# One evacuation, transpose and normalisation of the cross-attention sums per pair of sequences, with two heads in 32 rows, and weight clips at another step

## What is computed

```
x = layernorm(x + self_attention(x))          # 16 heads of 16 channels, causal
x = layernorm(x + cross_attention(x, ctx))    # works across channels, see below
x = layernorm(x + ffn(x))                     # 256 -> 1024 -> 256, activations and
                                              # weights quantised, silu, gelu, layernorm
```

```
scores = einsum('bhtc,bhsc->bhts', q, k) / sqrt(8)
p_attn = softmax(scores)
out    = einsum('bhts,bhsc->bhtc', p_attn, v)      # the value sums
out    = Wo @ out + bo
```

## Time and profile before

| what | us |
|---|---|
| median of three runs | 551.99 (551.63 to 553.26) |
| the profiled execution's own time | 549.98 |
| its span in the profile | 548.1 |
| stage 1 up to the last evacuation of `u_b` | about 408 |
| stage 2 | about 140 |

### The profile page before, as it was taken

How to read it: one execution, slowest core, us unless ns; L and a number is a source line. 1 busy time by engine, 2 the same in 40 slices (tenths; PEclk the granted TensorE clock), 3 DMA queues, 4 the chain that set the end, 5 groups by cost and what they waited for, 6 DMA issues and landing times. The chain is left out here.

```text
span 548.1 us, 12074 instructions
## 1 busy us (share of the span) xinstructions
PE 438.9 (80%) x4162; PEld 237.8 (43%) x4162; DVE 446.5 (81%) x980; ACT 383.8 (70%) x716; POOL 287.9 (53%) x389
## 2 busy tenths in 40 slices
PE   6568799999999999999999999998877602555564
PEld 4354445455455564545545455443332201333342
DVE  3755787988979889798998988888739959999983
ACT  2231266678777786777877768767878878999982
POOL 5742656455565555645547465551033637767652
PEclk9676799999999999999999999999998965555555
DMA  7135327342232322414223242221000000000001
GB/s 223 48 78 175 87 56 218 93 109 69 64 109 57 101 73 62 111 50 105 69 64 99 56 111 61 64 80 51 2 2 1 2 0 0 10 30 22 27 31 38
DMA packets 51676, 37.10 MB, mean 68 GB/s; under 512 B 21408, under 2 KB 47648, under 8 KB 51488
## 3 DMA queue, kind: packets, MB, share of 16 engines
q1 hardware_dynamic: 51328, 36.10, 23.2%
q10 hardware_dynamic: 288, 0.23, 0.2%
HBM read 24.52 MB, written 10.49 MB: 64 GB/s over the span
## 5 line engine op out<-in xcount | busy, mean ns | idle before, releaser
L980 DVE TENSOR_REDUCE MX<-mx_b 128x2 f32<-128x512 f32 x256 | 167.7, 678 | 29.2 <-PE mx_b L585 28.1
L785 ACT ACTIVATE PB<-e_b 128x512 f32<-128x512 f32 x256 | 149.4, 592 | 58.6 <-PE e_b L613 57.4
L585 PE MATMUL mx_b<-KA,QA 48*128 48x256 bf16 x512 | 97.5, 275 | 12.2 <-DVE MX L980 11.5
L613 PE MATMUL e_b<-QA,KA 50*128 50x256 bf16 x512 | 96.9, 274 | 0.3 <-DMA QA<-MR 0.3
L630 PE MATMUL u_b<-PB,VA 128*32 128x256 f32 x1024 | 82.6, 391 | 2.4 <-ACT PB L785 1.5
L907 POOL TENSOR_TENSOR SP<-SP,srec 128x1024 f32<-128x1024 f32 x15 | 28.5, 1903 | 81.1 <-DVE srec L952 81.1
L585 PEld LDWEIGHTS mx_b<-KA,QA 48*128 48x128 bf16 x512 | 29.4, 94 | 87.8 <-issue 43.9
L1308 PE MATMUL r_b<-identh,Q 128*128 128x128 f16 x128 | 16.6, 311 | 39.3 <-ACT Q L1221 39.3
L1253 POOL TENSOR_TENSOR H<-H,row_tab 128x1024 f32<-128x1024 f32 x15 | 35.4, 2360 | 21.4 <-ACT H L1211 17.9
L1314 PE MATMUL z_b<-w2q,Q2T 128*128 128x256 bf16 x128 | 30.2, 418 | 19.3 <-ACT Q2T L1232 19.3
L897 POOL TENSOR_TENSOR KM<-QK,att_tab 128x512 f32<-128x512 f32 x31 | 32.0, 1054 | 20.6 <-ACT QK L739 20.6
(11 more groups left out here) (172 smaller groups left out, 1050.5 us busy)
## 6 DMA issues: line engine op xcount, KB each, us to landing
KA<-parts_k SPq DMA_DIRECT2D x64, 96.0 KB
QA<-parts_q SPq DMA_DIRECT2D x64, 96.0 KB
parts_q<-part_q SPq DMA_DIRECT2D x32, 128.0 KB, 1.9
parts_k<-part_k SPq DMA_DIRECT2D x16, 192.0 KB, 2.1
C<-in_ctx SPq DMA_DIRECT2D x16, 128.0 KB, 3.1
X<-in_x SPq DMA_DIRECT2D x16, 128.0 KB, 3.2
out_y<-O SPq DMA_DIRECT2D x16, 128.0 KB, 1.7
XT<-in_xT SPq DMA_DIRECT2D x15, 128.0 KB, 2.2
```

Of the source, the lines that this page charges most:

```text
L585: m = nc.tensor.matmul(mx_b[n % 2][:, D * k:D * k + D], QA[low:low + K_MAX, 2 * i.ring + b, h, P * u:P * u + P], KA[low:low + K_MAX, 2 * i ...
L613: m = nc.tensor.matmul(e_b[n % 2][:, D * k:D * k + D], KA[low:low + K_EXP, 2 * i.ring + b, h, P * sc:P * sc + P], QA[low:low + K_EXP, 2 * ...
L785: nc.scalar.activation(PB[:, n % 4].rearrange("p e t -> p (e t)"), e_b[n % 2][:, :], ACT.Exp, scale=XC ** -0.5).then_inc(e_sb.sem, 1)
L980: nc.vector.tensor_reduce(MX[:, b, e, 2 * q:2 * q + 2, u], mx_b[n % 2][:, :].rearrange("p (e s) -> p e s", e=2), AXL.X, ALU.max).then_inc( ...
```

## The change

Heads j and 4 + j now share the same 32 rows of `u_b`, and a sequence takes 256 columns, so that the bank holds both sequences of the pair. For that `VA` gets zeros in columns 16 to 31 of each head (8 values, 8 ones, 16 zeros). Heads 0 to 3 take their own 32 columns as lhs, and heads 4 to 7 take 32 columns that begin 16 earlier, in the zeros of the head before. All four products of a head pair accumulate into the same place. `u_copy`, `u_transpose` and `u_norm` run once a pair, at step 0, 3 and 3 of the next turn, with a reciprocal of 32 and a product of 256 elements per partition. The channel order of the value bias and of the output weights is permuted on the host to match. The clips of turn 7's pieces and so on stand at step 1 of the following turn, all four together.

```diff
-        RD = sb("RD", [P, 16])
+        RD = sb("RD", [P, 32])
...
-        def u_transpose(pe, i, b, ps):
-            wait(pe, u_sb, i, b + 1)
+        def u_transpose(pe, i, ps):
+            wait(pe, u_sb, i, 1)
             for u in range(2):
-                for s4 in range(2):
-                    q = 2 * u + s4
-                    last = nc.tensor.transpose(ps[:, P * q:P * q + P], US[:, s4, P * u:P * u + P], ident)
+                for b in range(2):
+                    q = 2 * u + b
+                    last = nc.tensor.transpose(ps[:, P * q:P * q + P], US[:, b, P * u:P * u + P], ident)
...
+        def u_norm(dve, i, g):
+            wait(dve, ut_ps, i, 1)
+            sums = g_b[g][:, :].rearrange("p (n c) -> p n c", c=2 * XC)
+            if has(i, 1):
+                wait(dve, u_nrm, i.plus(-1), 2)
+                wait(dve, at_ps, i.plus(-1), 1)
+            nc.vector.reciprocal(RD[:].unsqueeze(2), sums[:, :, XC:XC + 1]).then_inc(u_nrm.sem, 1)
+            wait(dve, u_nrm, i, 1)
+            nc.vector.tensor_tensor(AN[:].rearrange("p u b (h c) -> p (u b h) c", c=XC), sums[:, :, 0:XC],
+                                    RD[:].unsqueeze(2).broadcast_to([P, 32, XC]), ALU.mult).then_inc(u_nrm.sem, 1)
...
                 if m % 4 == 0:
                     wait(pe, xv_sb, i, 1)
-                    if b == 1:
-                        wait(pe, u_sb, i, 1)
-                    elif has(i, 1):
-                        wait(pe, u_sb, i.plus(-1), 2)
+                    if b == 0 and has(i, 1):
+                        wait(pe, u_sb, i.plus(-1), 1)
                 wait(pe, e_sb, i, 2 * m + 2)
                 for j in range(4):
-                    last = nc.tensor.matmul(u_b[32 * j:32 * j + 32, D * s4:D * s4 + D],
-                                            VA[:, i.p, sc, b, 4 * s4 + j, :], PB[:, (2 * m + j % 2) % 4, j // 2, :],
-                                            start=sc == 0, stop=sc == 1)
+                    own = 32 * (4 * s4 + j) - 16 * s4
+                    last = nc.tensor.matmul(u_b[32 * j:32 * j + 32, D * b:D * b + D],
+                                            VA[:, i.p, sc, b].rearrange("p h c -> p (h c)")[:, own:own + 32],
+                                            PB[:, (2 * m + j % 2) % 4, j // 2, :],
+                                            start=s4 == 0 and sc == 0, stop=s4 == 1 and sc == 1)
...
-                    if s == 13 and real(i):
-                        u_transpose(pe, i, 0, use(g_b[1], u_nrm, i, 2))
...
-                    if s == 8 + int(i.v >= NPAIR - 2) and real(i):
-                        u_copy(i, 0)
...
-                    if s == 13 and real(i):
-                        u_norm(dve, i, 0, 1)
...
-                    if s in (6, 8, 13, 14) and W_ROUND <= i.v < W_ROUND + 4:
-                        weight_clip(2 * (i.v - W_ROUND) + s // 12, s in (8, 14))
+                    if s == 1 and W_ROUND <= i.v - 1 < W_ROUND + 4:
+                        for step in range(2):
+                            for piece in range(2):
+                                weight_clip(2 * (i.v - 1 - W_ROUND) + piece, step)
...
-            nc.gpsimd.memset(VA[:], 1.0).then_inc(s_ones, 1)
+            for half_cols, v in ((0, 1.0), (1, 0.0)):
+                nc.gpsimd.memset(VA[:].rearrange("p a s b h (z c) -> p (a s b h) z c", z=2)[:, :, half_cols], v).then_inc(s_ones, 1)
```

More of the change, by code:

```diff
@@ L278, in square_sum @@
                                  accum_out=sumsq[:, bass.ds(i.v, 1)]).then_inc(s_sq, 1)
-        def u_norm(dve, i, b, g):
-            wait(dve, ut_ps, i, b + 1)
-            sums = g_b[g][:, :].rearrange("p (u h c) -> p u h c", u=2, c=32)
-            if b == 1:
-                wait(dve, u_nrm, i, 2)
-            elif has(i, 1):
-                wait(dve, u_nrm, i.plus(-1), 4)
-                wait(dve, at_ps, i.plus(-1), 1)
-            nc.vector.reciprocal(RD[:].rearrange("p (u h) -> p u h", u=2).unsqueeze(3),
-                                 sums[:, :, :, XC:XC + 1]).then_inc(u_nrm.sem, 1)
-            wait(dve, u_nrm, i, 2 * b + 1)
-            nc.vector.tensor_tensor(AN[:, :, b, :].rearrange("p u (h c) -> p u h c", c=XC), sums[:, :, :, 0:XC],
-                                    RD[:].rearrange("p (u h) -> p u h", u=2).unsqueeze(3).broadcast_to([P, 2, XH, XC]),
-                                    ALU.mult).then_inc(u_nrm.sem, 1)
+        def u_norm(dve, i, g):
[3 more added lines that the diff above has]
+                wait(dve, u_nrm, i.plus(-1), 2)
+                wait(dve, at_ps, i.plus(-1), 1)
+            nc.vector.reciprocal(RD[:].unsqueeze(2), sums[:, :, XC:XC + 1]).then_inc(u_nrm.sem, 1)
+            wait(dve, u_nrm, i, 1)
+            nc.vector.tensor_tensor(AN[:].rearrange("p u b (h c) -> p (u b h) c", c=XC), sums[:, :, 0:XC],
+                                    RD[:].unsqueeze(2).broadcast_to([P, 32, XC]), ALU.mult).then_inc(u_nrm.sem, 1)
         def norm2_stats(dve, i, g):
@@ L786, in exp_tile, with u_copy @@
                                      scale=XC ** -0.5).then_inc(e_sb.sem, 1)
-            def u_copy(i, b):
-                wait(act, pv, i, 4 * b + 4)
-                if b == 1:
-                    wait(act, ut_ps, i, 1)
-                elif has(i, 1):
-                    wait(act, ut_ps, i.plus(-1), 2)
+            def u_copy(i):
+                wait(act, pv, i, 8)
+                if has(i, 1):
+                    wait(act, ut_ps, i.plus(-1), 1)
                 nc.scalar.activation(US[:].rearrange("p s t -> p (s t)"), u_b[:, :], ACT.Copy).then_inc(u_sb.sem, 1)
@@ L888, in _ @@
             bodies(act, body)
-            u_copy(Pair(0, NPAIR - 1), 1)
+            u_copy(Pair(0, NPAIR - 1))
         def k_mask(eng, ops, a, c, ev):
@@ L1026, in body @@
                     if s == 3 and real(prev):
-                        u_norm(dve, prev, 1, 2)
+                        u_norm(dve, prev, 2)
                     if s == 4 and fresh(a):
@@ L1317, in _ @@
             pe.wait_ge(s_tab, 4)
-            u_transpose(pe, last, 1, g_b[1])
+            u_transpose(pe, last, g_b[1])
             for t in range(TURNS1):
@@ L1470, in _ @@
                 if t == 1:
-                    u_norm(dve, last, 1, 1)
+                    u_norm(dve, last, 1)
                 if t == 4:
@@ L1533 @@
         for k, n in enumerate(XW):
-            cross_w[64 * b:64 * b + 64, k, split[b] if n in ROTATED else own] = weights[n].T
+            cross_w[64 * b:64 * b + 64, k, split[b] if n in ROTATED else own] = weights[n].T[packed] if n == "o" else weights[n].T
         for k, n in enumerate(XBIAS):
-            cross_b[split[b] if n in ROTATED else own, k] = biases[n]
+            cross_b[split[b] if n in ROTATED else own, k] = biases[n][packed] if n == "v" else biases[n]
     arrays = {
```

17 lines of the change are left out of this document (8 added, 9 removed).

## The result

| | before | after |
|---|---|---|
| median (us) | 552.47 (4 runs) | 539.91 (4 runs) |
| lowest and highest (us) | 551.63 to 553.26 (4 runs) | 538.75 to 540.41 (3 runs), and 548.92 |
| profiled execution (us) | 549.98 | 539.41 |
| its span (us) | 548.1 | 537.3 |

The account below looks back on a forecast made before the run. The prediction took TensorE's own list to bound the steady turns. Its terms, 6.4 + 1.35 + 2.4 − 0.15 = 10.0 us, gave 551.99 − 10.0 = 542.0 us, range 539.5 to 545.5, forecast chance 0.70.

Parts of the forecast that it names:

- the steady turns: Turns 1 to 5 and 7 to 12: step 13's transposes leave TensorE's list, 0.58 us each, 6.4 us in all.
- The clips: Leaving steps 6 to 14 of turns 7 to 10 gains 4 × 0.6 = 2.4 us; at step 1 they cost 0.
- `u_transpose`'s neighbours: Work around step 13 whose inputs come due earlier; all arrive in time, the closest by about 0.1 us.
- Turn 6: Weight total behind `self_pv` waits for the attention output's copy; 0.3 us gained, the middle of 0 and 0.58.
- rivals (a) to (d): (a) clips collide, 0.13; (b) waits swallow part of 0.58, 0.10; (c) VectorE sets pace, 0.04; (d) larger norm slows, 0.03.
- The evacuation on ScalarE and the fill on GpSimd: Step 8's evacuation and the two-piece `VA` fill: idle time on each engine covers them, counted as 0.
- the norm: `u_norm` at step 3 grows 0.15 us, covered by 0.41 us idle; uncovered for the last pair, −0.15 us.
- turn 14: VectorE bounds it around step 13; transposes and `u_norm` leave just behind TensorE's wait, 0.6 us gained.
- Turn 13: Its gain ends in the DMA wait for the last split queries; counted 0, bounds 0 and 0.58 us.
- turn 15: The evacuation of b = 0 leaves ScalarE and `pv_quad` no longer waits for it; 0.45 us gained.
- rival (d): Slower than before by step 3's larger norm, its input read at stride 16; 556 us at 1.4 us longer; chance 0.03.
- turn 0's gain: Meets turn 1's 0.5 us wait for the maxima rows' DMA; counted 0, bounds 0 and 0.58 us.

Follow-up runs that it names:

- the transposes put back: The changed kernel with four 128 x 128 transposes of the identity, read by nobody, added on TensorE at step 13; 546.09 us.
- the sums alone: The changed kernel with the weight clips put back at steps 6, 8, 13 and 14; 546.48 us, ratio 0.9881 to the kernel before.
- the reduction at step 3: The changed kernel with an extra VectorE reduction of 384 private elements behind `u_norm` at step 3; 547.27 us.
- the later total: The changed kernel with turn 6's weight total and its use on VectorE each one step later; 545.15 us, ratio 0.9846 to the kernel before.
- the later load: The changed kernel with the 1 MB load of `w2f` one turn later, on its own semaphore; 542.62 us, ratio 0.9797.
- the clips moved alone: The kernel before with only the weight clips moved to step 1 of the following turn; 550.42 us, ratio 0.9964.

## Why the prediction was off

**What held.** TensorE's list sets the steady turns (forecast 21.9, measured 21.91; the transposes put back cost all of it). The clips gave 4 × 0.59 (forecast 4 × 0.6), at 1.45 us for the four (1.4). Of `u_transpose`'s neighbours none became late, with 0.14 us left at the closest. Turn 6 gave 0.25 (forecast 0.3) for the reason named. None of the rivals (a) to (d) came true. The evacuation on ScalarE and the fill on GpSimd cost nothing that the turns show. The last pair's `u_transpose`, which closes stage 1, starts at 398.09 us where it started at 408.69 (forecast: near 398), and from there to the start of the last `x_out_proj` it is 3.97 us against 3.74, the larger norm's 0.23 where I had 0.15.

**What was mis-sized.** The reciprocal of 32 elements took 349 ns and not 265, because I had read 248 ns for 16 elements as nearly all fixed cost; the norm grew by 349 + 425 − 248 − 291 = 235 ns and not 150. In the steady turns the 0.41 us of idle time covered it still. In turn 14 it did not: TensorE now waits 0.28 us for it before `att_transpose`, and the DMA wait there grew from 0.52 to 0.65, so turn 14 gave 0.12 and not 0.6. Turn 13 gave 0.21 where I had 0, and turn 15 0.54 where I had 0.45; the three together 0.87 for a forecast of 1.05. Turns 0 and 1 gave 0.78 for 0.58: the DMA wait in turn 1 took back 0.40 (0.32 before, 0.72 after), not all of turn 0's 0.58. All errors together leave the turns' sum at 10.13 us against 10.15. That these cancel is luck; each is below 0.5 us.

Three readings on the way were wrong without moving the sum. The overlap of 0.08 us between clips is what was measured, but the row named for it (three reductions of 0.69 in 2.03) gives 0.02; the 1.4 us rest on a value that its row does not show. At 1.4 us more for the norm rival (d) would have been near 557 us, not 556. And a GpSimd product that had begun before the clip and kept its usual length was read as speaking against a whole block; it does not, as the last section says.

**What failed.** It is the last step, the way from the sum to the time: "The median before is 2.0 us above the profiled execution, and I keep that distance", and, for the range, "0.8 for the spread of a median of few runs". The sum of 10.0 us is right to a few tenths of the turns and 0.8 of the span. But the executions of one kernel scatter over far more than 0.8 us. The kernel before went from 549.05 to 558.27 us in 23 runs on one chip (to 555.47 without the highest), the kernel after from 539.63 to 546.86 and from 541.05 to 547.53 in 6 runs each. A median of three runs is not sure to be within 0.8 us of the true one when single runs lie 6.4 us apart or more, and the three runs after that count, 538.75 to 540.41, are among the five lowest of all sixteen; the fourth, 548.92, is the highest. The 2.0 us by which the median lay above the profiled execution did not hold either: in the three later measurements of the unchanged kernels the median lay 1.5, 3.6 and 0.2 us below it. Three measurements of the same kernel gave ratios of 0.9748, 0.9814 and 0.9822; the forecast, 542.0 / 551.99 = 0.9819, lies at the last two and outside the interval of the first. The prediction names no source for the 0.8; it was half of the 1.6 us that the three runs before spanned, and three runs show little of a spread.

Where the scatter sits can be read by comparing the traces of the same kernel. The kernel before, its second trace against the first (span 553.35 against 548.13 us): before turn 0 it is 1.74 us longer, in the turns 1.63, behind them 1.85. The kernel after, second against first (544.75 against 537.32): 0.59, 3.72 and 3.12; third against first (541.60): 0.87, 0.34 and 3.07. These are turn 14 of the kernel before and turn 15 of the kernel after in their second traces:

```profile
380.40:397.18 16.78, 14.52 (x150) 5.92 (x149) 13.29 (x27) 11.79 (x26) 1.01 (x3) 0.90 0.05 16
```

```profile
385.30:399.29 13.99, 13.78 (x105) 4.26 (x102) 4.92 (x15) 9.37 (x21) 3.60 (x4) 0.66 0.01 2
```

Turn 14 took 15.22 us at full clock and takes 16.78 at a mean clock of 0.90; turn 15 took 11.15 at 1.00 and takes 13.99 at 0.66. And this is stage 2 of the kernel after, from the last product of turn 15 to the end, in its first trace, then in its third:

```profile
394.98:537.32 142.34, 68.32 (x379) 37.36 (x376) 120.56 (x325) 116.32 (x140) 77.01 (x77) 0.63 0.05 15
```

```profile
396.19:541.60 145.41, 71.40 (x377) 39.46 (x376) 120.73 (x325) 116.36 (x140) 77.07 (x77) 0.60 0.04 15
```

The work of VectorE, ScalarE and GpSimd is the same to 0.2 us in both; TensorE's products take 3 us longer at a mean clock of 0.60 instead of 0.63, and the stage is 3 us longer. Over all thirteen traces stage 2 lasted 140.5 us at the highest mean clock (0.65) and 146.6 at the lowest (0.59). So the scatter at the end of the turns and in stage 2 comes from how long TensorE is granted 2.4 GHz and how long 1.2 GHz in stretches where its work is thin; turns 3 to 12 repeated to 0.01 us between traces of the same kernel. The whole executions say the same: of the sixteen of the kernel after, the six with a mean granted clock of 0.870 or more took 538.75 to 541.05 us, the four with 0.856 or less 546.86 to 548.92. The part before turn 0 is another matter: over the thirteen traces it lasts 65.90 to 68.79 us and does not follow the clock (66.85 us at 0.745, 68.78 at 0.752). What makes it longer stays open. No number in the profile of before gave the size of the scatter, and no edit touched it.

One bound of the sum was wrong for the same reason. I had bounded turn 0's gain by 0 and 0.58. In three of the kernels with the shorter turn 0 it was less than nothing. Turn 1 took 24.63 us with the sums alone, 25.28 with the reduction at step 3 and 25.05 with the later total; the second of these:

```profile
87.48:112.76 25.28, 23.33 (x236) 12.29 (x236) 19.77 (x38) 15.37 (x33) 12.06 (x18) 0.93 0.55 161
```

The wait for the DMA was 0.86, 1.38 and 1.34 us in them, and the clock then stood at half near 101 us for a while: these turns lost 1.7 to 2.4 us against the 22.90 of the first trace after. A wait of this size does not bring the fall each time: in the unchanged kernel's second trace TensorE waited 1.13 us in turn 1, and the clock stayed at full. In the traces of the kernels with the longer turn 0 and of those with the later load, turn 1 was at full clock. (With the clips moved alone it was turn 0 that came in at a mean clock of 0.90 and took 23.30 us: the clock rose late, behind the prologue.)

## What to carry over

In a loop as long as one engine's list, an instruction is worth the distance from its start to the next one's, once for each turn, and that can be forecast to a few hundredths; check the two or three results that come due earlier, and read the slack of an engine at the place that changes, not from its busy share. Before giving a range for a median, look for how far the executions of that kernel lie apart; where some stretches run at a clock that is granted or not, the spread of a few runs is a poor measure of it, and the range has to be wider than the errors of the sum. A small change is shown by the turns of two traces long before it is shown by medians.

## What was not expected of the hardware

- The reciprocal out of PSUM costs by the element: 248 ns for 16 and 349 for 32, so 101 / 16 = 6.3 ns for each more, where the product beside it went from 291 to 425 ns with 128 more, 1.05 ns for each. The Trainium skill's page VectorE: DVE Perf Modes, section First, the fixed hardware budget, describes the reciprocal as an iterative divide with a repeat count of 8; the ratio of 6 fits that, but no run here looks inside the reciprocal.
- A clip with GpSimd idle takes 0.41 us, single or in a row (each then begins 0.08 us before the end of the one ahead), where single ones beside GpSimd's products had taken 0.60 and 0.72. By the Trainium skill's page SBUF — State Buffer, section Who interferes with whom, whichever of two such instructions issues first shuts the other out for its whole length. The traces show that either side can be the longer one. In rows 9 GpSimd's product had begun 0.42 us before the clip, kept its 0.74, and the clip grew. With the sums alone, in each of turns 7 to 10, the clip began first, kept its 0.42, and GpSimd's product 0.08 us behind it took 0.92 instead of 0.74 (GpSimd's times are rough in a profile, but these repeat to 0.01 us in the four turns). Both agree with the page on who waits; the growth (0.19 us for 0.32 to 0.34 us side by side) is less than a whole shut-out would add. With the clips moved alone, in turns 8 to 10, a 128x1 instruction of GpSimd that began 0.09 us before the clips took 0.56 us instead of 0.27 and the clips did not grow, so the order of the starts in a trace does not settle it every time.
- The same kernel on the same chip lay 6.5 to 9 us apart from one execution to the next, mostly by the clock of its thin stretches. What starts a fall there stays open: a gap in TensorE's work alone is not it, since the 1.3 us gap of turn 14 stands in twelve traces and a fall follows its end within 0.4 us in three.
